# Layer 3 takes alpha from a column of the key product, and some turns are written anew

## The reference

```python
q = x @ Wq.T + bq
k = x @ Wk.T + bk
k = k / jnp.maximum(jnp.linalg.norm(k, axis=-1, keepdims=True), 1e-12)
v = x @ Wv.T + bv
alpha = jax.nn.sigmoid(x @ Wa.T + ba)      # one number for each token
beta = jax.nn.sigmoid(x @ Wb.T + bb)       # one number for each token
gate = jax.nn.sigmoid(x @ Wg.T + bg)
def step(S, inp):
    q_t, k_t, v_t, a_t, b_t = inp
    a = a_t[:, :, None]
    b = b_t[:, :, None]
    Sk = jnp.einsum('bij,bj->bi', S, k_t)
    S = a * (S - b * (Sk[:, :, None] * k_t[:, None, :])) + b * (v_t[:, :, None] * k_t[:, None, :])
    o = jnp.einsum('bi,bij->bj', q_t, S)
    return (S, o)
```

## Time and profile before

| | us |
|---|---|
| three timed runs | 1734.53, 1735.24, 1736.05 |
| the profiled execution | 1735.68 |
| its span, first to last instruction | 1733.9 |
| TensorE matmul busy | 1698.8 |
| VectorE busy | 1235.9 |
| GpSimd busy | 1218.6 |
| ScalarE busy | 1089.0 |

### The profile page before, as it was taken

One profiled execution on the slowest core, in us unless ns is written; L12 is line 12 of the kernel. 1 busy time (PEld: TensorE's weight loads), 2 busy tenths in 40 slices (PEclk: granted clock), 3 DMA queues, 4 the chain that ended last, 5 costly groups with the idle time before them and its releaser, 6 DMA issues.

```text
span 1733.9 us, 31801 instructions
## 1 busy us (share of the span) xinstructions
PE 1698.8 (98%) x10006; PEld 1302.2 (75%) x10006; DVE 1235.9 (71%) x4490; ACT 1089.0 (63%) x2904; POOL 1218.6 (70%) x1771
## 2 busy tenths in 40 slices
PE   8999999999999999999999999999999899999998
PEld 5888888876667676676676777767788787788976
DVE  7954335688977988988899866445566766578773
ACT  6555226456677678777777886546546666665656
POOL 5655549898878987888799785135347876666667
PEclk9999999999999999999999999999999999999999
DMA  7100000010000000000000000000000001000002
GB/s 254 68 32 1 1 1 4 3 51 1 1 1 1 1 1 1 1 1 1 1 1 1 1 11 6 1 1 7 2 3 3 1 18 31 21 2 1 2 3 73
DMA packets 24027, 26.70 MB, mean 15 GB/s; under 512 B 3492, under 2 KB 20772, under 8 KB 23476
## 3 DMA queue, kind: packets, MB, share of 16 engines
q1 hardware_dynamic: 23860, 24.67, 4.6%
HBM read 22.52 MB, written 2.15 MB: 14 GB/s over the span
## 4 chain that ended last, share of the span: by engine, by line
PE 84%; DVE 5%; POOL 5%; ACT 4%; issue 2%; POOLq 0%; DVEq 0%; ACTq 0%
PE ps L87 77%; PE ps L90 7%; POOL arena L104 5%; ACT arena L98 3%; DVE arena L104 2%; DVE arena L110 1%; DVE arena L147 1%; DVE arena L130 0%; ACT arena L99 0%; ACT L98 0%; DVE arena L133 0%; DVE arena L107 0%; DVE arena L136 0%; DVE ps L147 0%; DVE ps L104 0%
## 5 line engine op out<-in xcount | busy, mean ns | idle before, releaser
L104 POOL TENSOR_TENSOR arena<-arena 128x512 f32<-128x512 f32 (+6 forms) x836 | 715.4, 869 | 277.7 <-DVE arena L110 96.5
L98 ACT ACTIVATE arena<-ps 128x128 f32<-128x128 f32 (+11 forms) x1204 | 338.8, 326 | 393.5 <-PE ps L87 285.2
L87 PE MATMUL ps<-arena 128*128 128x128 f32 (+4 forms) x2792 | 440.5, 291 | 9.1 <-DVE arena L104 3.8
L87 PEld LDWEIGHTS ps<-arena 128*128 128x128 f32 x2792 | 373.4, 192 | 96.0 <-issue 47.6
L104 DVE TENSOR_TENSOR arena<-ps,arena 128x128 f32<-128x128 f32 (+4 forms) x696 | 313.2, 469 | 175.7 <-PE ps L87 163.4
L98 ACT ACTIVATE arena<-arena 128x128 f32<-128x128 f32 (+1 forms) x836 | 321.2, 439 | 50.9 <-POOL arena L104 38.9
L87 PE MATMUL ps<-arena,moe 128*128 128x256 f32 (+1 forms) x960 | 288.2, 439 | 0.0
L87 PE MATMUL ps<-arena,cst 128*128 128x504 f32 (+2 forms) x768 | 283.8, 489 | 2.4 <-ACT arena L98 1.3
L98 ACT ACTIVATE arena<-ps,cols 128x512 f32<-128x512 f32 x324 | 216.8, 688 | 103.2 <-PE ps L87 96.3
L104 POOL TENSOR_TENSOR arena<-arena,cst 128x144 f32<-128x144 f32 (+7 forms) x536 | 186.2, 356 | 92.4 <-ACT arena L98 57.7
L110 DVE SCALAR_TENSOR_TENSOR arena<-ps,arena 128x128 f32<-128x128 f32 (+1 forms) x476 | 157.0, 365 | 119.6 <-PE ps L87 94.1
(11 more groups left out here) (120 smaller groups left out, 1761.9 us busy)
## 6 DMA issues: line engine op xcount, KB each, us to landing
rows<-in_rows SPq DMA_DIRECT2D x1, 2253.0 KB, 14.5
arena<-in_x SPq DMA_DIRECT2D x8, 256.0 KB, 5.2
wf<-in_wf SPq DMA_DIRECT2D x2, 1024.0 KB, 7.0
arena<-in_L_ffn_W SPq DMA_DIRECT2D x8, 256.0 KB, 3.0
out_dram<-arena SPq DMA_DIRECT2D x8, 256.0 KB, 2.7
wmod<-in_wmod SPq DMA_DIRECT2D x4, 384.0 KB, 8.1
arena<-kept SPq DMA_DIRECT2D x24, 64.0 KB, 3.0
arena<-kept SPq DMA_DIRECT2D x8, 192.0 KB, 3.2
```

The source lines that it names most:

```text
L87: return UNSENT if self.e is None else self.e.matmul(out, lhsT, rhs, start=start, stop=stop)
L98: return self.e.activation(out, in_, func, bias=bias, scale=scale)
L104: return UNSENT if self.e is None else self.e.tensor_tensor(out, a, c, op)
```

## The change

Weights: `wa3` and `wkvb3` (257 columns) become one matrix `wkvba3` of 258 columns, whose last one is alpha's. The product `e3a` goes; each `e3k` product has 258 columns. ScalarE's sigmoid over 128x512 goes; for each tile it takes a sigmoid of column 257 to a column `al` of 128x1, ahead of beta's. After the four `e3k` products TensorE waits for all four columns and issues four transposes, each of a column broadcast to 128x128, so that row by row the bank holds alpha of the tile's tokens. VectorE does its adds for all four tiles first and then the eight scans, which read the PSUM bank; the second scan takes the identity as its other operand (which `bypass` ignores). The bank is freed by the last scan.

The turn strings: TensorE 3333 digits to 3303, VectorE 3861 to 3831, GpSimd 1180 to 1150, ScalarE 2145 to 2107. In each 30 are gone (6 for each of the five streams), and 8 more on ScalarE, whose generator has one turn fewer in each half. The rest is the same in outline. Counting the k-th turn of a stream in both strings, TensorE's turns move by 1 to 5 places on average in its first 500 turns, by 0.2 to 1.4 in the middle, and by 1 to 9 in the last 1000.

```diff
-                    ("wkvb3", 257), ("wa3", 1), ("wg3", 128), ("wo3", 128), ("wp1", 128), ("wp2", 8),
+                    ("wkvba3", 258), ("wg3", 128), ("wo3", 128), ("wp1", 128), ("wp2", 8),
...
-            self.ngcols = cc[:, 20:24]
-            self.arow, self.above = G[:, 0:512], self.XT
+            self.ngcols, self.al = cc[:, 20:24], cc[:, 24:28]
+            self.above = self.XT
...
-    "pe": ("2000000000000120002230001222000112200011100211012003013211003031110332001332322330320113213131222121"
+    "pe": ("0000000000020200022001022120013201120101001120012003011314000111303323200312321302333022313312112212"
...
                 pe.wait_ge(*at("e3h", b, g))
+                for i in range(4):
+                    yield
+                    ps = banks.take(pe, b, b, "e3k", g, i)
+                    pe.mm(ps[:, 0:258], m.hT[:, col4(i)], wsm("wkvba3")).then_inc(*pe.up(b, "e3k", b, g, i))
+                yield
                 ps = banks.take(pe, b, b, "e3a", g)
-                pe.mm(ps[:, :], wsm("wa3").broadcast_to([128, 128]), m.hT).then_inc(*pe.up(b, "e3a", b, g))
-                yield
-                for i in range(4):
-                    yield
-                    ps = banks.take(pe, b, b, "e3k", g, i)
-                    pe.mm(ps[:, 0:257], m.hT[:, col4(i)], wsm("wkvb3")).then_inc(*pe.up(b, "e3k", b, g, i))
+                pe.wait_ge(*at("e3al", b, g))
+                for i in range(4):
+                    ins = pe.tr(ps[:, col4(i)], m.al[:, i:i + 1].broadcast_to([128, 128]), ident)
+                ins.then_inc(*pe.up(b, "e3a", b, g))
...
-                ps = banks.get(b, "e3a", g)
-                act.wait_ge(*at("e3a", b, g))
-                act.act(m.arow, ps[:, :], ACT.Sigmoid, bias=row("ba3", 0, 1)).then_inc(
-                    *act.up(b, "e3arow", b, g, free=(b, "e3a", g)))
-                yield
                 for i in range(4):
                     yield
                     ps = banks.get(b, "e3k", g, i)
                     act.wait_ge(*at("e3kv", b, g, i))
+                    act.act(m.al[:, i:i + 1], ps[:, 257:258], ACT.Sigmoid, bias=row("ba3", 0, 1)).then_inc(
+                        *act.up(b, "e3al", b, g))
...
-                    yield
-                    dve.wait_ge(*at("e3arow", b, g))
-                    dve.scan(m.DT[:, c], m.arow[:, c], ident, 0.0, ALU.mult, ALU.add).then_inc(*dve.up(b))
-                    dve.scan(m.grow[:, c], m.arow[:, c], m.arow[:, c], 1.0, ALU.mult, ALU.bypass).then_inc(
-                        *dve.up(b, "e3scan", b, g))
+                ps = banks.get(b, "e3a", g)
+                for i in range(4):
+                    yield
+                    c = col4(i)
+                    dve.wait_ge(*at("e3a", b, g))
+                    dve.scan(m.DT[:, c], ps[:, c], ident, 0.0, ALU.mult, ALU.add).then_inc(*dve.up(b))
+                    dve.scan(m.grow[:, c], ps[:, c], ident, 1.0, ALU.mult, ALU.bypass).then_inc(
+                        *dve.up(b, "e3scan", b, g, free=(b, "e3a", g) if i == 3 else None))
```

More of the change, by code:

```diff
@@ L391 @@
 TURNS = {
-    "pe": ("2000000000000120002230001222000112200011100211012003013211003031110332001332322330320113213131222121"
[L393 to L421, removed]
-          "2322230212120011003011322100121103311003331132230320201122012102443311022311220120012110221313313231"
-          "1322103321223032213301330220013130213302213032213243013231323301131002310233122301301423012311203323"
-          "0122321322331234313231223232000020230232331113111031333120002121120221332023311133231010322033320002"
-          "220333312232322223333133000110211"),
@@ new lines @@
+    "pool": ("2041304020102010020023120001203011013320021443301231201302012103320313132102231101233111200200001223"
+          "3231200331200300002003033000002211221112222111110000111111011222222033200111112111122321111312003333"
+          "1102023322100001303103322033011100123322003332230230302222103322201020133133233012331012302123001021"
+          "2021333323113212302033122310003213111323030012333012302203213003233011120213311000222133212213303211"
+          "3301203122013210012130201321233213011102320003123300103222120330111213000112330231001003122201221012"
+          "2010313002011233303222133210012132200113201132203301023122232110311123303130213003133222031320220110"
+          "0203102302102200333203312110231221321123200111213002203320102000100031111311111131222222332322223223"
+          "0031003333300133333331333332211100000002000020220011110110312222031102230010032211223113221122322000"
+          "1200102013330010031330012302303233233013311031102112201132211022312123122132232211333213313301332033"
+          "3032033223303113000110300000201200232011013011033110112011001131222121332303322232033212301323321130"
+          "2323211022003100323202103230001200111123010312131002231212123021022133321123233310201232321333002313"
+          "30202311231023123001133221232323331101000223312233"),
@@ L2189, in l3_pe @@
                 pe.wait_ge(*at("e3h", b, g))
-                ps = banks.take(pe, b, b, "e3a", g)
-                pe.mm(ps[:, :], wsm("wa3").broadcast_to([128, 128]), m.hT).then_inc(*pe.up(b, "e3a", b, g))
-                yield
                 for i in range(4):
@@ L2195, in l3_pe @@
                     ps = banks.take(pe, b, b, "e3k", g, i)
-                    pe.mm(ps[:, 0:257], m.hT[:, col4(i)], wsm("wkvb3")).then_inc(*pe.up(b, "e3k", b, g, i))
+                    pe.mm(ps[:, 0:258], m.hT[:, col4(i)], wsm("wkvba3")).then_inc(*pe.up(b, "e3k", b, g, i))
+                yield
+                ps = banks.take(pe, b, b, "e3a", g)
+                pe.wait_ge(*at("e3al", b, g))
+                for i in range(4):
+                    ins = pe.tr(ps[:, col4(i)], m.al[:, i:i + 1].broadcast_to([128, 128]), ident)
+                ins.then_inc(*pe.up(b, "e3a", b, g))
                 yield
@@ L3093, in arrange @@
              "wread": i["L2_attn_W_read"].T, "wr2": i["L2_ffn_Wr"], "wq3": i["L3_attn_Wq"].T,
-             "wkvb3": np.concatenate([i["L3_attn_Wk"].T, i["L3_attn_Wv"].T, i["L3_attn_Wb"].T], 1),
-             "wa3": i["L3_attn_Wa"].T, "wg3": i["L3_attn_Wg"].T, "wo3": i["L3_attn_Wo"].T,
+             "wkvba3": np.concatenate([i["L3_attn_Wk"].T, i["L3_attn_Wv"].T, i["L3_attn_Wb"].T,
+                                       i["L3_attn_Wa"].T], 1),
+             "wg3": i["L3_attn_Wg"].T, "wo3": i["L3_attn_Wo"].T,
              "wp1": i["L3_ffn_Wp1"], "wp2": i["L3_ffn_Wp2"], "wo3f": i["L3_ffn_Wo"]}
```

167 lines of the change are left out of this document (94 added, 73 removed).

## The result

| | kernel before | changed kernel |
|---|---|---|
| timed runs, median (us) | 1736.04 (1734.53 to 1737.66) | 1743.72 (1740.79 to 1745.04) |
| ratio | | 1.0042, 95% interval 1.0032 to 1.0052 |
| profiled execution, span (us) | 1735.68, 1733.9 | 1740.79, 1739.0 |

The forecast was 1731, the range 1721 to 1741. The change costs 7.7 us by the medians and 5.1 us in the two profiled executions (that of the changed kernel is the fastest of its six). Where they lie is best read by the same matmul in both traces. The table gives the start of five matmuls, each the last of its kind, and the end of the span, as the difference to the kernel before in us; that kernel's own time is in the heading. The five are the last product of `wmod` with `sil`, the last product with 129 columns, the last transpose of `e3g`, the last product with 64 columns and the last matmul of all.

A forecast was written before the change was run, and what follows sets the result against it. TensorE, busy 98%, was taken as the bound. From the profiled execution, 1735.7 + 0.2 (TensorE's work) - 1.1 (chain) - 3.3 (turns) = 1731.5 us, put against the median as 1731 us, range 1721 to 1741.

The forecast's parts named there:

- I take a quarter, (12.1 + 1) / 4 = 3.3 us; the ends are -10 and +6 us: New turn strings on all four engines: reordering fills a quarter of TensorE's reachable idle, mostly behind 1350 us, gaining 3.3 us.
- the 5.1 us that the forecast had set aside: Kernel's end: 5.1 us of TensorE idle behind its last burst, left out of the idle a better order could touch.
- In TensorE's written order nothing is moved past a DMA: no queue of SP or GpSimd changes its instructions.: DMA queues: their instructions stay unchanged; the only new thing named is a stop at `e3a`.
- TensorE's work, +0.2 us: Layer 3, eight halves: four transposes replace one 512-column product, +0.02 us a half, 0.2 us in all.
- The chain of a half, -1.1 us, and idle of 3.3 us as its limit: Layer 3: each half gets 1.3 us shorter; TensorE idles only 3.3 us there, so a third counts, -1.1 us.
- work beside TensorE: Layer 3's scans on VectorE: even 4.2 us more from PSUM overhead would run beside TensorE, so zero was counted.
- VectorE, zero; the long scan: Layer 3's 64 scans from PSUM: -1.4 to +3.1 us, counted zero; the 1.25 us scan colliding with GpSimd should vanish.
- ScalarE, zero: Layer 3: 32 one-column sigmoids replace eight wide ones, -0.6 to +2.6 us, covered by TensorE's queue, counted zero.
- The new stop (the rival on the slow side): At `e3a` TensorE waits 0.8 us in each of 8 halves, +6.4 us, giving 1741 us; chance 0.21.
- Covered anyway: Rival: layer 3's streams already cover each other and TensorE's work stays within 0.2 us, so no change, 1735 us; chance 0.22.
- The granted clock is 1.00: TensorE throughout: clock 1.00, 0.99 at the end, so it runs at 2.4 GHz and nothing is to be had.
- What would show it: Trace signs: right if idle from 1350 us falls 4 us; wrong if transposes wait over 2 us or scans reach 0.5 us.

The follow-up runs named there:

- start_after: Kernel before with only the changed kernel's first-stage turns on all four engines, no code change: 1737.47 us, 1.0014 of the kernel before.
- start_before: Changed kernel with the kernel before's first-stage turns on all four engines: 1737.81 us, 1.0019 of the kernel before.
- out_first: Changed kernel with one VectorE turn, element 0's last add, moved ahead of turns for elements 2 and 3: 1737.64 us, 1.0018 of the kernel before.
- start_and_out: Changed kernel with both the kernel before's first-stage turns and element 0's last add earlier: 1736.49 us, 1.0005 of the kernel before.
- scan_sbuf: start_and_out with VectorE copying each half's alpha from PSUM to SBUF, where the scans read it: 1739.02 us, 1.0024 of the kernel before.
- tail_before: start_and_out with old turns from about 1628 us, SyncE's outputs in fitting order, its load waits ahead of them: 1733.95 us, 0.9996 of the kernel before.
- before_sp: Kernel before with SyncE's outputs issued in order of their last adds, waits for loads ahead of them: 1733.45 us, 0.9995 of the kernel before.
- work_back: start_and_out plus an unread 512-column product ahead of each half's new transposes: 1741.72 us, 1.0035 of the kernel before.
- work_less: start_and_out with 128 of 258 columns left out of each of 32 products, output wrong: 1733.59 us, 0.9995 of the kernel before.

## Why the prediction was wrong, step by step

- **"I take a quarter, (12.1 + 1) / 4 = 3.3 us; the ends are -10 and +6 us".** This step failed, by its sign and its place. It priced the new strings by the idle time behind 1350 us that a better order could fill, and took a gain of 3.3 us where the turns of two places cost 0.37%, 6.4 us. These are the turns of the first stage (2.4 us alone by start_after, 4.0 by start_before; VectorE's first 60 are enough) and VectorE's last add of element 0 (4.2 us by out_first). The first lies ahead of 1350 us, the second behind the last matmul, in the 5.1 us that the forecast had set aside. The end is dear because SyncE's issues follow in a fixed order. Why the start is dear isn't settled: TensorE stops for `mcols`, and in the profiled executions the 1.2 GHz level stands there too, but the kernel before has that level as well, and the mean clock of start_after's timed executions is hardly lower.
- **"In TensorE's written order nothing is moved past a DMA: no queue of SP or GpSimd changes its instructions."** True of the instructions and wrong as a conclusion. The outputs' issues wait for VectorE's adds in element order, so a moved add moves seven of them. The 5.1 us behind the last burst were set aside, and not asked what sets them.
- **TensorE's work, +0.2 us.** Mis-sized. It comes to 8 x (0.44 - 0.86) = -3.4 us. The eight records in 0.88 us of the earlier trace rows were eight transposes, not four; I had taken two records each. That an fp32 matmul appears as two records holds for the products and not for the transposes.
- **The chain of a half, -1.1 us, and idle of 3.3 us as its limit.** From the end of layer 2 to the last `e3g` 2.3 us were won in the changed kernel, 2.4 in start_and_out. TensorE had 3.4 us less to do there, so no run shows that the shorter chain as such gave anything. scan_sbuf shows that this stretch hangs on VectorE too: work added to VectorE there, which the forecast called "work beside TensorE", cost 4.3 us. From the last `e3g` to the last matmul 2.2 us are given back. tail_before, a spliced order, didn't keep them either. What would keep the gain is left open; a search of that tail's turns for this front wasn't tried.
- **VectorE, zero; the long scan.** Right. No scan passes 424 ns. By the Trainium skill (SBUF — State Buffer, Who interferes with whom) a VectorE instruction with two SBUF inputs contends with a GpSimd instruction that reads SBUF, and one with at most one SBUF input, outside the 2-port modes, doesn't. The traces of three kernels agree: 396 to 424 ns with one input in PSUM, up to 1249 before and up to 618 in scan_sbuf, where both are in SBUF. The 60 and 125 ns of overhead that the Trainium skill gives for SBUF and PSUM (Perfetto Trace Analysis, Optimizing Scalar/DVE Operations) don't show as a difference here: the medians are 398 ns from PSUM and 400 and 416 from SBUF.
- **ScalarE, zero.** Nothing speaks against it: 116.5 us busy from 1450 to 1630 us, before 116.7.
- **The new stop (the rival on the slow side).** Its time, 1741, was nearest by luck, its mechanism is refuted. All 322 transposes from 1450 to 1630 us, the new ones among them, have 1.2 us of idle time ahead of them, where the stop needed 6.4 us in sum and the prediction's sign for it 2 us.
- **Covered anyway.** This is what layer 3 did in sum, by start_and_out at 1.0005. It would have been right of the code and not of the change. Its reason, TensorE's work the same within 0.2 us, was off: 3.4 us went.
- **"The granted clock is 1.00".** Of the first 20 us this was misread: by the record lengths of the kernel before, TensorE was at the 1.2 GHz level there for some 10 us, and before_sp, which wasn't, is 3.4 us ahead from there on.
- **What would show it.** The sentence "a difference that sits before 1000 us, where only turns changed" named one of the two places. None named the queue of the outputs.

## What to carry to other kernels

Where an order is written out by hand or by a search, look first at its two ends: the engine that waits for the first inputs, and the queue that issues the outputs. A turn moved a few places cost up to 4.2 us there, while through the middle of this kernel, from 100 to 1414 us, the new strings moved the changed kernel by 0.3 us. Compare two traces by the same instruction in both, from start to end; busy shares would have shown nothing here, since TensorE's differ by 0.4 us. And cut and add work on the same engine before calling it the bound: added work cost its full time here, and seven tenths of a deep cut brought nothing.

## What the runs showed of the hardware

- An fp32 transpose of 128 columns takes 0.11 us in a burst (four in 0.44 us) and leaves one record; an fp32 product leaves two, 0.86 us for 512 columns, 0.215 us for each 128. Per column a transpose costs half.
- Output DMAs issued one behind another on SyncE took 0.44 to 0.92 us each from one start to the next; seven of them were 5.05 us.
- Waits of SyncE whose semaphores had long been met took 0.06 us each: 52 of them 3.1 us at the end of the kernel before.
- In each kernel with the new start or a part of it TensorE stood 1.2 to 3.7 us near 8 us, and the granted clock from 10 to 18 us was 0.50 to 0.59; records of 384 columns took 844 ns there instead of 486. With the old start TensorE stood 0.4 to 1.6 us (in the kernel before not at all), and the clock was 0.91 to 1.00 in five profiled executions, 0.79 in work_back, 0.67 in scan_sbuf and 0.50 in work_less; in the kernel before it reads 1.00 while the records have the length of 0.50. So in these traces the lower level comes more often with the new start, and the old start doesn't exclude it. One execution each doesn't show that the stop brings it: before_sp stood 1.61 us and stayed at 1.00, work_less stood 1.22 us at 0.50.
